# A grouped convolution with a channel shuffle: the shuffle as whole transposes, and the shuffled image in another layout

## The reference, cut to what matters

```python
x = x + L0(gn(x))       # gn: group normalization, 32 groups of 16 channels
x = x + L1(gn(x))

# L0: 3x3 convolution in 8 groups of 64 channels; then, inside each group,
out = out.reshape(B, G, gout, L).transpose(0, 1, 3, 2)   # (64, 1024) -> (1024, 64)
out = out.reshape(B, G * gout, Ho, Wo)                   # read as (64, 1024) again

# L1: 512 -> 128 channels (1x1), normalization, relu = h;
#     18 offsets by a 3x3 convolution of h;
#     deformable 3x3 convolution of h: 9 taps, 4 neighbours each;
#     normalization; 128 -> 512 channels (1x1); normalization; relu
```

## Time and profile before

| | us |
|---|---|
| median of 3 runs | 2210.93 |
| lowest and highest | 2209.67 and 2238.08 |
| the profiled execution | 2238.84 |
| its span, first to last instruction | 2236.9 |

### The profile page before, as it was taken

How to read it: one execution, slowest core, us unless ns; L and a number is a source line. 1 busy time by engine, 2 the same in 40 slices (tenths; PEclk the granted TensorE clock), 3 DMA queues, 4 the chain that set the end, 5 groups by cost and what they waited for, 6 DMA issues and landing times.

```text
span 2236.9 us, 31922 instructions
## 1 busy us (share of the span) xinstructions
PE 1810.2 (81%) x10144; PEld 995.9 (45%) x10144; DVE 1395.2 (62%) x3450; ACT 966.5 (43%) x1475; POOL 1182.4 (53%) x1160
## 2 busy tenths in 40 slices
PE   5988787897889788788887888789788878887544
PEld 2544443544545454444444444454444445443221
DVE  5537566574757658466674857668476665846554
ACT  6545353353545435354353545345354443522211
POOL 0046555564556546555564555556455554655664
PEclk9989898897989889888897989899798988988877
DMA  5055665575665656666575665657566575565664
GB/s 181 6 188 154 207 201 179 148 235 173 196 204 169 231 151 219 188 193 194 148 238 164 203 197 181 217 162 238 165 203 199 163 232 156 176 203 160 211 198 154
DMA packets 142933, 412.94 MB, mean 185 GB/s; under 512 B 24614, under 2 KB 25126, under 8 KB 142758
## 3 DMA queue, kind: packets, MB, share of 16 engines
q0 software_dynamic: 92160, 302.06, 45.7%
q1 hardware_dynamic: 50598, 108.71, 13.1%
HBM read 339.37 MB, written 71.30 MB: 184 GB/s over the span
## 4 chain that ended last, share of the span: by engine, by line
PE 47%; DVE 15%; another core or an unknown queue 15%; issue 13%; ACT 5%; POOL 2%; DMA 1%; SPq 1%; ACTq 0%; DVEq 0%; POOLq 0%
PE bank L775 14%; PE bank L757 8%; PE bank L789 8%; DVE sb_rows L567 5%; PE bank L843 4%; PE bank L748 4%; DVE sb_val L575 4%; PE bank L764 3%; PE bank L865 3%; PE bank L808 2%; DVE sb_split L608 2%; POOL sb_rows L332 2%; DVE sb_raw L623 1%; ACT sb_split L406 1%
## 5 line engine op out<-in xcount | busy, mean ns | idle before, releaser
L332 POOL DMA_INDIRECT sb_rows<-table,sb_ridx x1152 | 1178.0, 1023 | 1011.7 <-DVE sb_val L575 440.5
L775 PE MATMUL bank<-sb_split,sb_wg 128*128 128x512 f16 x2304 | 602.5, 409 | 29.6 <-ACT sb_conv_sb L378 20.2
L567 DVE SCALAR_TENSOR_TENSOR sb_rows<-sb_rows,sb_frac 128x256 f32<-128x256 f32 x1152 | 488.3, 479 | 73.6 <-DMA sb_rows<-table,sb_ridx 50.5
L575 DVE SCALAR_TENSOR_TENSOR sb_val<-sb_rows,sb_frac 128x128 f32<-128x128 f32 x1152 | 328.6, 347 | 178.5 <-remote 140.3
L789 PE MATMUL bank<-sb_fold_sb,sb_conv_sb 128*64 128x64 f32 x4096 | 307.1, 287 | 124.6 <-issue 120.3
L775 PEld LDWEIGHTS bank<-sb_split,sb_wg 128*128 128x128 f16 x2304 | 231.2, 104 | 366.3 <-issue 152.9
L616 DVE TENSOR_TENSOR sb_xs<-bank,sb_xs 128x512 f32<-128x512 f32 x128 | 88.3, 690 | 477.4 <-remote 324.6
L757 PE MATMUL bank<-sb_valT,sb_wd 128*128 128x512 f32 x576 | 365.7, 719 | 15.7 <-issue 11.3
L360 ACT ACTIVATE sb_valT<-bank 128x512 f32<-128x512 f32 x288 | 171.2, 595 | 407.5 <-remote 249.1
L789 PEld LDWEIGHTS bank<-sb_fold_sb,sb_conv_sb 128*64 128x64 f32 x4096 | 271.0, 206 | 166.9 <-issue 161.1
L378 ACT ACTIVATE sb_conv_sb<-bank,sb_bias 128x512 f32<-128x512 f32 x256 | 173.6, 685 | 387.7 <-PE bank L775 219.2
(11 more groups left out here) (77 smaller groups left out, 1095.3 us busy)
## 6 DMA issues: line engine op xcount, KB each, us to landing
table<-sb_table_sb SPq DMA_DIRECT2D x144, 256.0 KB
sb_xs<-x SPq DMA_DIRECT2D x64, 512.0 KB
out<-sb_res SPq DMA_DIRECT2D x128, 256.0 KB
sb_rows<-table,sb_ridx POOLq DMA_INDIRECT x1152
sb_rows<-w_group SPq DMA_DIRECT2D x8, 288.0 KB, 9.3
sb_wd<-w_def SPq DMA_DIRECT2D x1, 576.0 KB
sb_w<-w_in SPq DMA_DIRECT2D x1, 256.0 KB
sb_w<-w_out SPq DMA_DIRECT2D x1, 256.0 KB
```

Of the source, the lines that this page charges most:

```text
L332: pool.indirect_dma_start(out=rows[:, (c % RING) * PER + i, :], out_offset=None, in_=tables[u % 2], in_offset=bass.IndirectOffsetOnAxis(ap ...
L567: op = nc.vector.scalar_tensor_tensor(r[:, 0:2 * CH], r[:, 2 * CH:4 * CH], frac[:, parity, half * PER + i, k, 0:1], r[:, 0:2 * CH], ALU.mu ...
L575: op = nc.vector.scalar_tensor_tensor(val[:, c % 2, i * CH:(i + 1) * CH], r[:, CH:2 * CH], frac[:, parity, half * PER + i, k, 1:2], r[:, 0 ...
L775: op = nc.tensor.matmul(pair_ps[half][:, :], wg[:, g, k, :], plane(split1[:, g, :], ky + half * HROWS, kx, HROWS), start=k == 0, stop=k == ...
```

## The change

It moves the image that has been shuffled to another layout and splits the two uses of x.

- x is loaded twice: to one buffer `xc` (channel x pixel) for the first normalization, and to one of three buffers `xl` for the shuffle and the residual. `xl` has 64 x half and channel on the partitions, and group and 512 pixels in the free dimension. The load of `xc` stands behind the output store of slot 17; those of `xl` in slots 12, 14, 16 and 4, each behind the landing of the store that frees its place.
- The group convolution has its two groups of a pair side by side: matmuls of 128 x 64 weights, one to partitions 0 to 63 and one to 64 to 127, first with the 9 high taps, then with the 9 low ones on top in PSUM (18 + 18 matmuls where 9 + 9 were). Its sum is complete, so it is evicted half as often, with the pixels sorted (written with a stride of 512 bytes).
- The shuffle is 8 transposes of 128 x 128 a call, of contiguous columns.
- The input product contracts 64 rows in each half, the output product gives 64 columns for each half. One pair of output products a slot, in slots 9 to 16, after both halves are done.
- x + relu is summed in place in `xl` and stored from there. The loop is two rounds of six steps.

```diff
-    XBUFS = 4
+    XBUFS = 3
+    CYCLE = 6
...
+        OUT_CONV = {9: 0, 10: 1, 11: 2, 12: 3, 13: 4, 14: 5, 15: 6, 16: 7}
+        STORE = {11: 0, 13: 1, 15: 2, 17: 3}
+        RELOAD = {12: 0, 14: 1, 16: 2}
+        RELOAD_LAST = 4
...
# SyncE, head of a step
+                        sp.wait_ge(norm1_done, count(3 * QUADS, new, 3 * (q + 1 - QUADS)))
+                        sp.dma_start(xc[:, q, :], x[bass.ds(new, 1), q].rearrange("a p n -> (a p) n"))\
+                          .then_inc(xc_loaded[q], 16)
...
# SyncE, slots of STORE and RELOAD
+                        sp.wait_ge(sum_done, count(GROUPS, t - 1, 2 * q + 2))
...
+                            sp.wait_ge(stored[q], count(32, t - 1, 32))
...
+                        load_shuffled(new, (u + 2) % XBUFS, q)
...
# ScalarE
-                act.wait_ge(stored[q], count(32, image, 16 * half))
-                nc.scalar.activation(res[:, q, :], out_ps[:, :], ACT.Relu, bias=bn_t[:, 2 + q:3 + q],
+                act.wait_ge(sum_done, count(GROUPS, image, g - 1))
+                nc.scalar.activation(res[:, g % 2, :], out_ps[:, :], ACT.Relu, bias=bn_t[:, 2 + g:3 + g],
...
+                by_place = conv_sb[:, q % 2, :].rearrange("p (j h c) -> p c h j", h=2, j=COLS // 2)
+                nc.scalar.activation(by_place[:, half * (GIN // 2):(half + 1) * (GIN // 2)],
...
+                    for g in (2 * q, 2 * q + 1):
+                        w = slice(g * CH, (g + 1) * CH)
+                        op = nc.scalar.activation(w1_norm[:, w], w1[:, w], ACT.Identity, scale=gs2[:, 3, g:g + 1])
...
# TensorE
+                for half in (0, 1):
+                    op = nc.tensor.matmul(out_ps[64 * half:64 * half + 64, :], w2[:, g * GIN:(g + 1) * GIN],
+                                          mid[:, half, :], start=True, stop=True)
...
                 for k in range(TAPS):
                     ky, kx = divmod(k, 3)
-                    op = nc.tensor.matmul(pair_ps[half][:, :], wg[:, g, k, :],
-                                          plane(split1[:, g, :], ky + half * HROWS, kx, HROWS),
-                                          start=k == 0, stop=k == TAPS - 1)
+                    for e in (0, 1):
+                        op = nc.tensor.matmul(pair_ps[half][64 * e:64 * e + 64, :],
+                                              wg[:, 2 * q + e, k, part * GIN:(part + 1) * GIN],
+                                              plane(split1[:, 2 * q + e, :], ky + half * HROWS, kx, HROWS),
+                                              start=part == k == 0, stop=part == 1 and k == TAPS - 1)
...
-                for jj in range(COLS // 2):
-                    for e in (0, 1):
-                        j = half * (COLS // 2) + jj
-                        op = nc.tensor.matmul(
-                            shuf_ps[half][64 * e:64 * e + 64, jj * GIN:(jj + 1) * GIN],
-                            conv_sb[:, (2 * q + e) % 3, j:j + COLS * (GIN - 1) + 1:COLS], fold_sb[:, :],
-                            start=True, stop=True)
+                for jj in range(COLS // 4):
+                    j = part * (COLS // 4) + jj
+                    op = nc.tensor.transpose(dst[:, jj], conv_sb[:, q % 2, j * 128:(j + 1) * 128], eye_sb[:, :])
...
+                            p = slice(64 * half, 64 * half + 64)
+                            op = nc.tensor.matmul(pair_ps[half][:, :], w1_norm[p, g * CH:(g + 1) * CH],
+                                                  xl[p, (u + 1) % XBUFS, g, :], start=g == 0, stop=g == GROUPS - 1)
```

321 lines of the change are left out of this document (172 added, 149 removed).

## The result

The changed kernel takes 2212.28 us (median of 20 runs, 2184.03 to 2232.65), the kernel before beside it 2232.53 (20 runs): a ratio of 0.9886, with a 95% interval of 0.985 to 0.9921. The ratio leaves out runs more than 1.5% above the fastest of the same kernel, and the profiled execution of the changed kernel is one of these. It is faster by 20 us by the medians (25 by the ratio), about 1%, where 125 were forecast. (The forecast of 2086 started from the 2211 of three runs; twenty have 2232.53.) The profiled execution took 2227.42 us, its span 2225.6.

What follows compares the result with a forecast made beforehand. TensorE was taken to bound the kernel, with 19.9 us an image lost around the dense shuffles. Terms of -7.0 an image gave -95, start -20, end +12 and -10: total -125, a 2086 us median; range 1940 to 2270.

Steps and rivals of the forecast that it cites:

- Stalls, -14 an image: TensorE's stalls around the shuffle: half the instruction density removes 7.5 + 6.2 us an image, leaving 6.
- the stalls belong to the gathers: Rival for the stalls around the shuffle: all 20 us an image stay, 2275 us; chance 0.10.
- Shuffle, -7.8: Shuffle: 8 calls an image, each eight transposes in 0.98 us where it took 1.96; saves 7.8 us an image.
- Convolution, +3: Convolution: 16 runs an image of 18 half-width matmuls, 2.1 us for 1.99, plus changes of shape; +3 us an image.
- Output, input and bias products, +4.6: Products split into halves that overlap only partly in float32: output +2.8, input +0.9, bias +0.9 us an image.
- the move: Four output products move from slots 0 to 3 to slots 13 to 16; +1.7 us an image.
- the waits: Output product's waits for a relu that waited for a store of `res`: no longer needed, -1 us an image.
- x, +5: Later load of x: ScalarE's first sum waits about 2.5 us, table stores queue 2.5 behind it, an image.
- ScalarE, +1.5: Slot 10's eviction behind a relu, about 1; longer weight scaling in slot 13, 0.5; strided eviction no change; us an image.
- The end, -10: End of the kernel: waits for stores go, -10 us, against +12 for eight output products in a row, not four.
- The first three steps: Start of the kernel: convolution and shuffle run without gathers' stalls in full; an estimated -20 us.

Runs made afterwards that it cites:

- joined pairs: The kernel before with its shuffle's matmuls joined in pairs, 8 in place of 16 a call; ratio 0.9933.
- the two folding shuffles: The kernel before with shuffle matmuls joined in pairs, 0.9933; the changed kernel with nine full convolution matmuls, eight folding shuffle matmuls, reordered eviction, 1.0109.

## Why the prediction was wrong

- **Stalls, -14 an image: the step that failed.** It charged the stalls to the shuffle's density, because "issue" stood in front of one kind of instruction. Without gathers there are next to none in either kernel ("issue" 6.0 and 10.5); with them "issue" on TensorE is 250 before and 261 to 331 after, so the term was worth nothing. The rival "the stalls belong to the gathers" was right and had a chance of 0.10. Its price, 2275, was 63 us too high, as it kept the other terms. What should have told was there: the slow matmuls of the earlier trace rows lie in a stall that the chain of the kernel before has from 1082.15 to 1090.26, and GpSimd's timeline has twelve gathers in an unbroken row over the same time. The first two rows below are of that chain, the others of that timeline.

```profile
1082.15 1.09 issue
...
1090.26 1.89 PE bank L775 x4
```

```profile
1073.33 1.03 POOL L332 DMA_INDIRECT sb_rows<-table,sb_ridx  x1 [5.84 <-DVE sb_val L575]
...
1087.24 0.95 POOL L332 DMA_INDIRECT sb_rows<-table,sb_ridx  x1 [0.30 <-issue]
1094.72 0.94 POOL L332 DMA_INDIRECT sb_rows<-table,sb_ridx  x1 [6.53 <-DVE sb_val L575]
```

  Nine us into the row TensorE stalls, and 2 us after its last gather it runs at full speed again; in the changed kernel it was 13 and 2 us.
- **That work on the chain is time.** The earlier trace rows gave TensorE 47% of the chain, but 28% were "issue" and unknown queue. With whole transposes alone TensorE's share fell to 30%, and VectorE's and the unknown queue's rose to 24% and 23%. Of 249 us of TensorE's busy time, some 110 became time. That these shares fall on whichever engine is due fits, but is argued.
- **Shuffle, -7.8.** Right by accident. A call has four transposes, not the eight that the step counted (COLS // 4 in the diff); they end 0.43 behind the transposes before them (1039.42 - 1038.99 below, TensorE's timeline of the changed kernel), not 0.98. TensorE saved 12.2 an image, of which 7.6 to 9.9 (122 to 158, over 16) became time without gathers.

```profile
1038.33 0.66 PE L785 MATMUL bank<-sb_eye_sb,sb_val 128*128 128x128 f32 x4
1038.82 0.60 PE L833 MATMUL bank<-sb_eye_sb,sb_conv_sb 128*128 128x128 f32 x4
```

- **Convolution, +3.** 2.11 a run where undisturbed, as worked out (2.1); 40 / 16 = 2.5 an image without gathers.
- **Output, input and bias products, +4.6.** Too high for the output: the 512 instructions of the halves take 159.3 us where 256 of full width took 154.9, so halves in float32 run beside each other. The Trainium skill, "TensorEngine Tiling (Array Packing)", Key Properties, says that of tiles; the trace agrees. On the chain a pair takes 1.10 (2199.76 below) where 1.2 was worked out.
- **All of the rest** (these, the move, the waits, x, ScalarE: 4.6 + 1.7 - 1 + 5 + 1.5 = 11.8) measured 3.3 to 5.6 without gathers (53 to 90, over 16) and 48 / 16 = 3.0 with them. Within it, *x, +5*: the waits came (60.1 us of ScalarE's), but taking them away gained nothing that can be told. *ScalarE, +1.5*: taking "no change" for the strided eviction was the wrong end; it went to 1149 ns. The Trainium skill, "SBUF — State Buffer", Door 1, has a penalty for strides past 16 bytes; the trace agrees, 1149 against 685 ns. It cost 16 to 27 us where the text worked out 10 from a doubling.
- **The end, -10.** It grew. From the end of the last unknown wait to the last instruction it was 2236.9 - 2215.0 = 21.9 us and is 2225.6 - 2192.7 = 32.9, while the wait went only from 10.56 to 5.62: together +6. The wait, and the first and the last of the eight output products, in the chain after:

```profile
2187.07 5.62 another core or an unknown queue
...
2199.76 1.10 PE bank L802 x4
...
2217.68 2.00 PE bank L802 x4
```

  The granted clock is 1.00 (2.4 GHz) from 2199.0 to 2203.5, where TensorE was busy for 2.16 us of 4.50, and 0.50 (1.2 GHz) from 2205 to 2220, where a pair takes 2.00. The first three steps were to give 20: image 2's first table copy starts at 349.3 us before and 345.6 after.
- In sum, with the stalls at nothing the prediction's own terms give +7.0 an image, a slower kernel; it came out faster as the rest cost 3 to 6 where 11.8 were counted. That 2212 lies between 1940 and 2270 is owed to the width of that range. Without gathers the parts give -122 + 40 + 53 = -29 us, and with them, between two lots, -111 + 17 + 48 = -46. Both sums come out as the whole change does in the same lots by the way they are made, so they say where the time went and don't prove the parts one by one.

## What to carry to other kernels

Before a stall is charged to the instruction that it stands in front of, ask what else runs during all of its microseconds and ends with it: here the unbroken rows of gathers. A lookahead is a cost, too: being allowed three chunks of gathers ahead instead of two cost 0.032 here (0.9685 against 0.9362, in two lots), more than the whole change gained. And here, where 28% of the chain belonged to no engine, TensorE's saved work was worth less than half of itself (110 of 249 us).

## What the runs showed of the hardware that was not expected

- Long unbroken rows of GpSimd's gathers go with stalls of TensorE, which begin 8.9 us or later in a row of the changed kernel. The chain's unknown queue, 13% there, is 0% with half of the gathers. Their bytes don't matter (302.06 or 75.57 MB), and the time isn't in proportion to their number: half of them gives 1681 us, none 1674, all 2226 in the lot of the half. With pauses between the gathers TensorE's "issue" is 13.7 us. What stands behind it, GpSimd's issuing or something in the DMA queues, isn't shown.
- The page's instruction queue q8 has 81 packets of 16 KB in the changed kernel and 62 with whole transposes in the kernel before, with "issue" of 261.2 and 232.4 us. The price of a packet isn't fixed: 3.2 us in the changed kernel, 2.8 in the one before (90 packets), 1.7 with joined pairs (72). The Trainium skill, "Runtime: NRT & Kernel Launch", Instruction fetch mechanics, calls crossing such a block "mostly hidden". Without gathers the trace agrees (80 packets, 10.5 us); with them it would not, if the stalls are refills, which no run here proves. For it: in the changed kernel 18 of the 27 stalls begin 0.5 to 3.5 us after a packet of q8 starts, and such stretches are 11% of the span. Against it: in the kernel before only 9 of 32 do (12%), and in the stall shown a packet starts at 1150.48 and none moves from 1151.9 to 1161.4, while TensorE still stalls.
- 128 weight columns that lie 64 bytes apart take 310 ns to load, contiguous ones 199 ns (means of the two folding shuffles).
